# Attention scores from folded keys: one 99-row product, and row maxima over 1024 columns in one instruction

## What is computed

```python
c_q = h_t @ W_DQ + b_DQ                      # (4, 1024, 32)
c_kv = h_t @ W_DKV + b_DKV                   # (4, 1024, 32)
q_c = (c_q @ W_UQ + b_UQ)                    # 8 heads of 128
k_c = (c_kv @ W_UK + b_UK)
v_c = (c_kv @ W_UV + b_UV)
q_r = (c_q @ W_QR + b_QR)                    # 8 heads of 32
k_r = h_t @ W_KR + b_KR                      # 32, shared by the heads
scores = (q_c . k_c + q_r . k_r) / sqrt(160)
o = softmax(scores) @ v_c
```

## Time and profile before

| | us |
|---|---|
| Median of 3 runs | 1002.3 (1001.36 to 1002.73) |
| The profiled execution | 1002.61 |
| Its span | 1000.9 |
| Attention: first to last score matmul | 106.1 to 594.1 |

### The profile page before, as it was taken

How to read it: one execution, slowest core, us unless ns; L and a number is a source line. 1 busy time by engine, 2 the same in 40 slices (tenths; PEclk the granted TensorE clock), 3 DMA queues, 4 the chain that set the end, 5 groups by cost and what they waited for, 6 DMA issues and landing times. The chain is left out here.

```text
span 1000.9 us, 21467 instructions
## 1 busy us (share of the span) xinstructions
PE 881.8 (88%) x8406; PEld 527.7 (53%) x8406; DVE 713.9 (71%) x1315; ACT 588.0 (59%) x1004; POOL 655.7 (66%) x437
## 2 busy tenths in 40 slices
PE   4893899999999999999999988962499999999995
PEld 1350244444444444444444547862266777677764
DVE  4768888888888888888898836872075666566643
ACT  3750577777777777777777663664265446544650
POOL 4200599999999999999999993698404524442452
PEclk9995799999999999999999998985599999999998
DMA  9910000000000000000000004259525434543110
GB/s 279 339 43 0 1 2 2 2 2 2 2 2 2 2 2 2 2 2 2 2 2 1 3 1 169 99 198 320 201 69 162 143 107 140 175 142 123 43 52 19
DMA packets 48166, 71.61 MB, mean 72 GB/s; under 512 B 7508, under 2 KB 40473, under 8 KB 47938
## 3 DMA queue, kind: packets, MB, share of 16 engines
q1 hardware_dynamic: 38114, 53.13, 16.1%
q0 software_dynamic: 7680, 16.87, 5.2%
q10 hardware_dynamic: 2272, 0.24, 0.2%
HBM read 46.76 MB, written 29.67 MB: 76 GB/s over the span
## 5 line engine op out<-in xcount | busy, mean ns | idle before, releaser
L834 POOL TENSOR_TENSOR prob_lo<-prob 128x1024 f16<-128x1024 f32 x208 | 437.3, 2130 | 95.0 <-ACT prob L799 94.9
L799 ACT ACTIVATE prob<-st_ps 128x512 f32<-128x512 f32 x512 | 301.4, 597 | 131.8 <-PE st_ps L723 129.5
L859 DVE TENSOR_REDUCE part_max<-x_ps 128x1 f32<-128x512 f32 x512 | 325.1, 678 | 66.7 <-PE x_ps L733 65.7
L722 PE MATMUL st_ps<-QA,KA 128*128 128x512 f16 x512 | 198.1, 387 | 0.5 <-ACT prob L799 0.5
L723 PE MATMUL st_ps<-QB,KB 65*128 65x512 f16 x512 | 196.4, 384 | 0.0
L771 PE MATMUL acc_ps<-VV,prob 128*128 128x65 f16 x2048 | 159.3, 194 | 3.9 <-POOL prob_lo L834 3.9
L771 PEld LDWEIGHTS acc_ps<-VV,prob 128*128 128x128 bf16 x2048 | 143.6, 98 | 33.4 <-POOL prob_lo L834 6.1
L771 PE MATMUL acc_ps<-VV,prob_lo 128*128 128x65 f16 x2048 | 158.7, 194 | 0.0
L771 PEld LDWEIGHTS acc_ps<-VV,prob_lo 128*128 128x128 f16 x2048 | 134.9, 98 | 29.9
L1340 POOL DMA_INDIRECT out<-yo,xb x48 | 47.7, 993 | 153.3 <-DVE yo L1447 151.1
L732 PE MATMUL x_ps<-KA,QA 64*128 64x512 f16 x256 | 102.2, 399 | 20.8 <-DVE part_max L859 20.7
(11 more groups left out here) (177 smaller groups left out, 1346.7 us busy)
## 6 DMA issues: line engine op xcount, KB each, us to landing
w1f<-in_L_ffn_w SPq DMA_DIRECT2D x8, 1024.0 KB, 6.1
w2f<-in_L_ffn_w SPq DMA_DIRECT2D x8, 1024.0 KB, 6.1
xbuf<-zeros SPq DMA_DIRECT2D x7, 910.0 KB, 16.7
xb<-xbuf SPq DMA_DIRECT2D x8, 780.0 KB, 5.4
x<-in_L_attn_h_t SPq DMA_DIRECT2D x8, 512.0 KB, 8.9
out<-x SPq DMA_DIRECT2D x4, 1024.0 KB, 5.9
tbuf<-x SPq DMA_DIRECT2D x4, 1024.0 KB, 9.7
tbuf<-gb_row SPq DMA_DIRECT2D x4, 1024.0 KB, 4.7
```

The source lines that it names most:

```text
L722: mm(st_ps[i % 2][:], KA[:, at], QA[:, n % QRING, half], start=True, stop=False)
L799: nc.scalar.activation(prob[:, k, f * HALF:(f + 1) * HALF], st_ps[i % 2][:], ACT.Exp).then_inc(exp_done, 1)
L834: nc.gpsimd.tensor_tensor(prob_lo[:, k, :], prob[:, k, :], prob_top[:, k, :], ALU.subtract).then_inc(sub_pool, 1)
L859: nc.vector.tensor_reduce(part_max[:, n % 2, item // 2, item % 2:item % 2 + 1], x_ps[i % 3][:], AX.X, ALU.max).then_inc(smax_done, 1)
```

## The change

The head's matrix moves from the queries to the keys. For each head the keys' latent features are multiplied by the head's matrix (`keys`: four matmuls, `GH` with `KA` and `GL` with `KB`) into 98 rows x 1024 columns in PSUM. ScalarE copies them as fp16 into `KX`, VectorE subtracts for rows 64 to 96 to get the low part there, and row 98 of `KX` is -1. `CQ` itself is then the queries' side for all heads, with the row of maxima as its 99th row; it exists twice, for even and odd heads.

- Scores of a half: one matmul of 99 rows (`KX`, `CQ`) for two.
- Maxima of a query tile: two matmuls of 98 rows one after the other, into one `x_ps` of 1024 columns, and one `tensor_reduce` over 1024 columns. The stationary operand is every eighth query. `x_ps` has two buffers; the keys' product uses one of them, between maximum 4 and maximum 6.
- `part_max`, L866, L758, L809 and `mrow` go: the DMA takes `mz` (128x8) directly to the row.
- `by_vector(n)`: (6,) for every fourth head, (4, 6) for the others.
- Preparation: `side(FOLD)` and `side(FOLD + 1)` with 16 small fp32 products each instead of eight, VectorE's `GH` and `GL` instead of `GQ`; `KC` goes; `CQ` is copied once by DMA at the start of the attention.

```diff
-        def by_vector(n):
-            return (5, 7) if n % 2 else (5,)
+            return (6,) if n % 4 == 3 else (4, 6)
...
+        def place_of_maxima(n, j):
+            return (9 * n + j + (j > KEY_SLOT)) % 2
+        def place_of_keys(n):
+            return (9 * (n - 1) + KEY_SLOT + 1) % 2
...  SyncE
+                sp.dma_start(CQ[0:QROWS, 1, :], CQ[0:QROWS, 0, :]).then_inc(copied, 16)
                 for n in range(HEADS):
-                    sp.wait_ge(mrow_done, n + 1)
-                    sp.dma_start(QB[LR:LR + 1, n % QRING, :].rearrange("a (t q) -> a t q", q=P),
-                                 mrow[:, n % 2, :]).then_inc(mrow_in[n % 2], 16)
+                    b = n // H
+                    sp.wait_ge(smax_done, ST * (n + 1))
+                    if n >= 2:
+                        sp.wait_ge(scores_ready, 2 * ST * (n - 1))
+                    sp.dma_start(CQ[QROWS:QROWS + 1, n % 2, b * S:(b + 1) * S].rearrange("a (g t) -> a g t", t=ST),
+                                 mz[:, n % 2, :]).then_inc(mrow_in[n % 2], 16)
...  TensorE: scores
-                    mm(st_ps[i % 2][:], KA[:, at], QA[:, n % QRING, half], start=True, stop=False)
-                    mm(st_ps[i % 2][:], KB[:, at], QB[:, n % QRING, half], start=False, stop=True).then_inc(scores_ready, 1)
+                    mm(st_ps[i % 2][:], KX[:, n % KRING, k * P:(k + 1) * P],
+                       CQ[:, n % 2, b * S + f * HALF:b * S + (f + 1) * HALF], start=True, stop=True).then_inc(scores_ready, 1)
...  TensorE: maxima
+                    if j == 0:
+                        te.wait_ge(kl_done, n + 1)
+                        if n == 1:
+                            te.wait_ge(copied, 16)
+                    if j == KEY_SLOT + 1:
+                        te.wait_ge(smax_done, ST * n + j)
+                    elif j == KEY_SLOT + 2:
+                        if is_head(n + 1):
+                            te.wait_ge(kl_done, n + 2)
+                    elif ST * n + j >= 2:
+                        te.wait_ge(smax_done, ST * n + j - 1)
+                    bank = x_ps[place_of_maxima(n, j)]
+                    for f in HALVES:
+                        half = slice(f * HALF, (f + 1) * HALF)
+                        last = mm(bank[:, half], queries_of[:, n % 2, b * P:(b + 1) * P, j], KX[0:QROWS, n % KRING, half],
+                                  start=True, stop=True)
+                    last.then_inc(smax_ready, 1)
...
+                def keys(n):
+                    b, h = n // H, n % H
+                    if n:
+                        te.wait_ge(smax_done, ST * (n - 1) + KEY_SLOT)
+                    bank = x_ps[place_of_keys(n)]
+                    for f in HALVES:
+                        mm(bank[0:QROWS, f * HALF:(f + 1) * HALF], GH[:, h, :],
+                           KA[:, b * S + f * HALF:b * S + (f + 1) * HALF], start=True, stop=False)
+                    for f in HALVES:
+                        last = mm(bank[0:QROWS, f * HALF:(f + 1) * HALF], GL[:, h, :],
+                                  KB[:, b * S + f * HALF:b * S + (f + 1) * HALF], start=False, stop=True)
+                    last.then_inc(k_ready, 1)
...  ScalarE
+                    nc.scalar.activation(KX[0:QROWS, n % KRING, :], x_ps[place_of_keys(n)][0:QROWS, :], ACT.Copy).then_inc(kh_done, 1)
...  VectorE
+                    nc.vector.tensor_reduce(mz[:, n % 2, j:j + 1], x_ps[place_of_maxima(n, j)][:],
                                             AX.X, ALU.max).then_inc(smax_done, 1)
...
+                def keys_low(n):
+                    v.wait_ge(kh_done, n + 1)
+                    at = KX[LR:QROWS - 1, n % KRING, :]
+                    nc.vector.tensor_tensor(at, x_ps[place_of_keys(n)][LR:QROWS - 1, :], at, ALU.subtract).then_inc(kl_done, 1)
...
                 for p, k in slots():
                     if k == ST - 1 and is_head(p):
                         add_halves(p)
+                    if is_head(p + 2):
+                        maxima(p + 2, k)
+                    if k == KEY_SLOT + 1 and is_head(p + 3):
+                        keys_low(p + 3)
                     ns, ks = scores_of(p, k - 1) if k else (-1, 0)
                     if is_head(ns) and ks in by_vector(ns):
                         subtract(ns, ks)
```

## The result

The changed kernel takes 1069.7 us in the median of four runs (1067.6 to 1071.7), the kernel before 1001.9 in the same comparison: ratio 1.068, 95% interval 1.065 to 1.070. It is slower, as predicted, but by 68 us instead of 24, and outside the range of 980 to 1058.

A forecast was written before the change was run, and what follows sets the result against it. TensorE set the pace before; after the change VectorE's chain with its waits, including those at GpSimd, would. 1002.6 + 21.9 (heads) + 2 (attention's start) = 1026.5 us, range 980 to 1058.

The forecast's parts named there:

- TensorE stops being the bound: TensorE's work in the attention falls to 1.36 us a slot and 11.7 us a head instead of 15.
- VectorE's work: VectorE's operations per head, with 1024-column reductions at 1.135 us: 12.9 us with two subtractions, 11.8 with one.
- (a): VectorE's wait before reduction 5: maximum 5 needs maximum 4's place, so its matmuls wait for reduction 4; 0.79 us.
- (b): VectorE's wait before reduction 6: maximum 6 takes the keys' place after the keys' low part; 0.79 us.
- (c): VectorE's wait before `both`: TensorE, held at maximum 6, still has the scores and values of slots 6 and 7; 0.72 us.
- The subtraction that waits for GpSimd: VectorE's first subtraction in a head waits for GpSimd's running one: +1.3 us with two subtractions, +0.9 with one; second none.
- B: Rival: VectorE's subtractions do not wait at GpSimd; 15.2 and 14.1 us a head, 992 us (984 to 1000); chance 0.25.
- The sum: Over 29 head periods, 22 x 16.5 + 7 x 15.0 = 468.0 against 446.1 us: +21.9 us.
- D: Rival: TensorE's clock drops between maxima 4 and 6, +1.85 us a head; 1079 us in every head, 1052 half; chance 0.15.
- The start of the attention: First maximum also waits for ScalarE's copy and the keys' low part, with hand-overs at 1.2 GHz: +2 us (0 to +4).
- The rest and the tail: DMA of the maxima row hidden by 1.7 us; preparation 0 (-1 to +1.5); GpSimd's tail after the heads 0 +- 1 us.
- Rival E: Loads of every eighth query, a 16-byte step, take 0.4 us: +1.1 us a head, 1058 us; chance 0.05.

The follow-up runs named there:

- e4: Changed kernel plus 23 unread matmuls a head before TensorE's waits, and VectorE's subtraction replaced by a reduction (low parts of tiles 4 and 6 left out): 1008.3 us.
- e14: Changed kernel, same share of subtractions, plus unread matmuls only where TensorE stands in each kind of head and ahead of the first head: 1031.0 us.
- e10: Changed kernel with one VectorE subtraction a head (tile 6), 14 unread matmuls a head and 4 before each of the first maxima pairs: 996.2 us.
- e7_fill_m6: Changed kernel plus only the 8 unread matmuls a head before maximum 6: 1041.4 us.
- e6_fill_m4: Changed kernel plus only the unread matmuls of slot 4, 10 before maximum 4 and 2 before the keys: 1055.9 us.
- e1_no_share: Changed kernel with VectorE's subtraction replaced by a one-input reduction, low parts of tiles 4 and 6 left out: 1024.1 us.
- e11: As e10, but VectorE subtracts tile 7 in place of tile 6, right before reduction 5: 993.4 us.
- e9_no_keys: Changed kernel with 16 unread matmuls a head and keys made for heads 0 to 2 only, reused by the others: 957.2 us.

## Why the prediction was right and wrong

- *TensorE stops being the bound* and *VectorE's work*: right. A maxima pair in series takes 0.43 to 0.44 when the clock is up (403.67 to the score matmul at 404.10; 0.49 right behind a wait). A reduction of 1024 columns is spaced 1.12 to 1.13 (three in 3.35, 402.11 to 405.46; two in 2.27, 408.09 to 410.36). Before another operation that waits it counts its full 1.23, which I had only partly. So with the clock at 1.00 a head with two subtractions has 16.7 - 3.4 = 13.3 us of work on VectorE against 12.9, and 3.44 of waits against 3.6; the two errors partly cancel to the 0.15 us a head by which the sum was low.
- *Waits (a), (b), (c)*: right in place and size, 0.75, 0.75 and 0.66 against 0.79, 0.79 and 0.72, where the clock is full.
- *The subtraction that waits for GpSimd*: right. 1.28 in heads with two (predicted 1.3), 0.65 in heads with one (0.9), nothing at the second. B, the other side, assumed that it does not happen; e4, in which it cannot, came to 1008, so even then it would not have been faster than before with those added matmuls. The Trainium skill, SBUF — State Buffer, SBUF: two separate sides, calls the pair's use an exclusive lock that a VectorE operation with two SBUF inputs and a GpSimd operation take for a whole instruction; the rows agree (end of GpSimd's + 1.12), and the keys' low part, with one PSUM input, takes 1.227 to 1.228 in all 32 cases.
- *The sum* failed in one term, the clock. The prediction put it at nothing in the sum and had it only as a rival, with a chance of 0.15. That rival had the mechanism and, for a drop that reaches (c), nearly the price: +1.85 a head, measured +2.0 to 2.3. But it priced no other place. Against the 16.7 and 15.1 of e14, the changed kernel's heads with two subtractions are longer by 0.4 to 0.8 in 16 cases (10 us in all, in most of them the drop behind maximum 4 that lengthens (a)) and by 2.2 to 2.7 in five (12 us, the drop that reaches (c)); the seven with one are longer by 0.5 to 1.6 (9 us), and the last period by 2.0. The rows spoke louder than a chance of 0.15. The earlier trace rows had 1.00 at TensorE busy 58.7 of 60 us and 0.58 at 2.46 of 5, and nothing between; the forecast's own numbers gave TensorE 11.7 of 16.5 us, far below the first, and 3.4 in 6.5 from maximum 4 to maximum 6. There was no row that said it would stay up. The clock cost 33.0 / 29 = 1.14 us a head on average. D's sizes for every head (1079; its terms add up to 1080) and for half of them (1052, by its terms 1053) lay on both sides of the 1069.7 measured, but that is luck: in most heads another and cheaper wait was the one that grew. The range took in only half of D and so ended at 1058.
- *The start of the attention*: +2 predicted, +8.3 measured. The reason I gave (one more hand-over at 1.2 GHz) brought the first score matmul from 106.11 to 108.14, as predicted. The other 6 us lie behind it: before, the clock was 1.00 from 118 on; now it stayed down or fell again,

```profile
114.00:122.00 8.00, 6.95 (x32) 3.13 (x33) 4.69 (x5) 3.71 (x7) 5.46 (x3) 0.57 0.01 0
...
130.00:138.00 8.00, 7.15 (x68) 4.47 (x67) 4.06 (x4) 3.68 (x6) 3.79 (x3) 0.50 0.01 2
```

  so most of it is the same missing term. In e10, with the clock up, the first `both` comes 46.8 us after the first keys' product (84.29), in the kernel before 44.8 after the first query product (85.99): +2.0 for a head 0 with one subtraction, and by my estimate some +3.6 with two (1.6 more, the 16.7 against 15.1 of e14's heads). The changed kernel has 53.9, so about 1.6 of what was missed is that second subtraction, which the +2 left out, and 5.5 the clock.
- *The rest and the tail*: right for the rest. The DMA of the maxima hid, the preparation moved by less than 1 us. The end was 2.4 us shorter, outside 0 +- 1.
- *Rival E*: the load with a 16-byte step is longer, 144 ns against 98 for the one with a 4-byte step:

```profile
L737 PEld LDWEIGHTS x_ps<-KX,CQ x512: 140/144/174, 89.7 to 643.5; 98*128 98x128 f16 x171
```

  but it lies beside the matmul before it, and the pair stays at 0.43 to 0.44. A contiguous operand was not tried, so this rests on these rows.

Together: the direction and the account of VectorE, GpSimd and the hand-overs hold (e14: 1031.0 against the forecast's 1026.5), and 39 of the 43 us missed are the difference between the changed kernel and e14. The step that failed is the sum's silence on TensorE's clock: the sum took 1.00 throughout, and the changed kernel's trace shows 0.89 over the 29 head periods. Why the clock falls in one head and not in the next with the same work stays open.

## What to carry to other kernels

When a change takes work off a full TensorE and makes it wait on another engine's results, its clock belongs in the sum, not among the rivals, unless a row shows it full with such waits in the queue. Price it at the place where it falls: 2.0 to 2.3 us a head where two slots of TensorE's work stood between VectorE and its next input, 0.7 where one did, and not in every head. A few matmuls whose result is not read, placed just ahead of such a wait, gave back 39 us here, but only where TensorE stands anyway; where it no longer stands they cost 0.5 us a head.

## What the runs showed of the hardware

- TensorE fell to 1.2 GHz in 26 of the first 28 head periods of the changed kernel, though it never stood longer in them than 1.7 us between two matmuls: 1.47 us before maximum 4, up to 1.66 before maximum 6. The same standing was not always followed by a drop. e7_fill_m6 kept a clock of 1.00 over eleven heads and lost it in later ones, and in e6_fill_m4 12 of 21 heads with two subtractions kept it behind 1.66 us.
- A wait at GpSimd makes a second cost where TensorE depends on the waiting engine: TensorE stood 1.47 us before maximum 4 in the changed kernel and not in e1_no_share. The wait was worth 46 us with the clock left alone, and at least 27 with it held.
- VectorE's subtraction ended 1.12 to 1.13 us after the GpSimd subtraction during which it arrived, so the earlier it arrived in it the longer it waited: 1.14 us when it came 0.63 into it (e11), 0.65 when it came 1.12 into it (e10). What matters is the place within GpSimd's running instruction, not how much either engine has to do.
- GpSimd's `o_n` is held up by VectorE's subtraction as its own subtractions are: 1.59 us in e9_no_keys in place of 0.61.
